# Chunk sums moved to GpSimd, and the next step's attention started inside a lone step

## What is computed

```
pooled = x.reshape(B, C, 14, 16, 14, 16).sum(axis=(3, 5))       # 16x16 patch sums
h = einsum('bcij,ce->bije', pooled, channel_weights)            # 196 tokens of 192
h = h + attention(layernorm(h))      # 12 heads; weights relu(1 + qk + qk^2 / 2), normalised
h = h + experts(layernorm(h))        # 8 experts 192 -> 768 -> 192, the best 2 of each token
```

## Time and profile before

| | |
|---|---|
| median of 3 runs | 1360.76 us (1356.45 to 1372.45) |
| span of the profiled execution | 1353.8 us |
| busy share of the span | PE 91%, PEld 81%, DVE 71%, ACT 44%, POOL 44% |
| DMA | 284.42 MB, mean 210 GB/s |
| mean granted TensorE clock | 0.937 |

### The profile page before, as it was taken

One profiled execution on the slowest core, in us unless ns is written; L12 is line 12 of the kernel. 1 busy time (PEld: TensorE's weight loads), 2 busy tenths in 40 slices (PEclk: granted clock), 3 DMA queues, 4 the chain that ended last, 5 costly groups with the idle time before them and its releaser, 6 DMA issues.

```text
span 1353.8 us, 26903 instructions
## 1 busy us (share of the span) xinstructions
PE 1228.0 (91%) x7299; PEld 1093.9 (81%) x7299; DVE 956.8 (71%) x3407; ACT 596.2 (44%) x1127; POOL 600.4 (44%) x483
## 2 busy tenths in 40 slices
PE   5867766999999999899999899999999979999997
PEld 3756655888888888788888788888888879998996
DVE  6799998787878787877787687868783523333454
ACT  1221223454545454445444354535454534544664
POOL 0104333425454454453644545464555464533433
PEclk9986556999999999898999899989999989999999
DMA  9679887767878887778786878877744655544555
GB/s 354 231 254 347 320 281 262 231 220 240 238 232 221 255 216 245 204 238 218 234 246 217 210 237 234 250 208 234 195 129 80 211 117 130 107 95 89 119 142 112
DMA packets 126551, 284.42 MB, mean 210 GB/s; under 512 B 24819, under 2 KB 70500, under 8 KB 126500
## 3 DMA queue, kind: packets, MB, share of 16 engines
q1 hardware_dynamic: 82762, 241.95, 54.5%
q0 software_dynamic: 43104, 41.25, 17.7%
q10 hardware_dynamic: 634, 0.61, 0.2%
HBM read 228.79 MB, written 54.95 MB: 210 GB/s over the span
## 4 chain that ended last, share of the span: by engine, by line
PE 33%; DMA 19%; DVE 17%; POOL 15%; issue 14%; ACT 1%; POOLq 1%; SPq 0%; ACTq 0%; DVEq 0%
PE ps L993 11%; DMA result<-ys,ridx 11%; PE ps L962 10%; POOL rows_d L608 8%; DMA rows_d<-rows,sloti 7%; POOL result L623 7%; DVE red L1069 6%; PE ps L802 3%; PE ps L933 2%; PE ps L934 2%; DMA w1r<-L_attn_w_qkv 1%; DVE stats L1197 1%; DVE topi L1206 1%; PE ps L1022 1%; DMA xr<-rows_d 1%
## 5 line engine op out<-in xcount | busy, mean ns | idle before, releaser
L623 POOL DMA_INDIRECT result<-ys,ridx x210 | 333.1, 1586 | 307.9 <-issue 120.4
L993 PE MATMUL ps<-w2a,hid 128*128 x2520 | 455.5, 327 | 0.0
L608 POOL DMA_INDIRECT rows_d<-rows,sloti x256 | 258.9, 1011 | 394.0 <-DMA rows_d<-rows,sloti 146.7
L993 PEld LDWEIGHTS ps<-w2a,hid 128*128 128x128 f32 x2520 | 415.4, 190 | 11.8 <-issue 0.2
L1069 DVE TENSOR_REDUCE red<-xbuf 128x21 f32<-128x672 f32 x448 | 359.2, 841 | 5.3 <-PE ps L866 2.4
L727 ACT ACTIVATE hid<-ps,b1s 128x512 f32<-128x512 f32 (+1 forms) x344 | 222.9, 654 | 239.2 <-PE ps L962 230.5
L962 PE MATMUL ps<-xh,w1h 128*128 128x512 f32 (+1 forms) x344 | 166.0, 482 | 7.9 <-DVE xl L1306 3.9
L1329 DVE TENSOR_TENSOR w1l<-w1r,w1h 128x768 fp32r<-128x768 f32 x116 | 110.3, 951 | 70.9 <-ACT w1h L739 70.3
L962 PE MATMUL ps<-xh,w1l 128*128 128x512 f32 (+1 forms) x344 | 131.5, 382 | 0.0
L962 PE MATMUL ps<-xb,w1h 128*128 128x512 f32 (+1 forms) x344 | 131.3, 382 | 0.0
L962 PE MATMUL ps<-xl,w1h 128*128 128x512 f32 (+1 forms) x344 | 131.2, 381 | 0.0
(11 more groups left out here) (164 smaller groups left out, 1633.8 us busy)
## 6 DMA issues: line engine op xcount, KB each, us to landing
xbuf<-x SPq DMA_DIRECT2D x224, 672.0 KB, 5.6
w1r<-L_ffn_w SPq DMA_DIRECT2D x118, 384.0 KB, 3.7
xr<-rows_d SPq DMA_DIRECT2D x48, 402.0 KB, 3.4
result<-h1s SPq DMA_DIRECT2D x32, 294.0 KB
w2a<-L_ffn_w SPq DMA_DIRECT2D x8, 576.0 KB, 7.6
rows_d<-rows,sloti POOLq DMA_INDIRECT x256
rows_d<-pad SPq DMA_DIRECT2D x9, 402.0 KB, 4.6
result<-ys,ridx POOLq DMA_INDIRECT x210, 4.9
```

The costliest lines, as they stand in the source:

```text
L608: pool.indirect_dma_start(rows_d, bass.IndirectOffsetOnAxis(ap=sloti[:, k * NT + t:k * NT + t + 1], axis=0), rows[:, t, :], None).then_inc ...
L623: pool.indirect_dma_start(out, bass.IndirectOffsetOnAxis(ap=ridx[:, b, n:n + 1], axis=0), ys[:, b, n, :], None, compute_op=ALU.add).then_i ...
L993: last = mm(yout(g, b, n), hid[:, m % 3, cols], w, start=False, stop=m == MC - 1 and n % 2 == 1)
```

## The change

Three things change, all of them ahead of the loop.

GpSimd sums some chunks: 2, 5, 8, 11 of step 0's x during the setup, the seven odd ones of step 1's x while the setup ends, then 4, 6, 9, 11 of the x of steps 2, 3 and 4 among the scatters of the lone steps 0, 1 and 2, and also 12 and 13 of step 4's x in step 3. One chunk is five additions, each of which adds the upper half of the runs to the lower half and waits for the one before. Who waits for a chunk (SP, PE) now waits for both counts.

In the lists, `T1` and `T2` now stand ahead of `S8`, the new `T3` (the next step's `S3`) behind it, and `T4` (the next step's `S4`) among the `V`s. The moments and turned features of the next step go to banks 3 to 5, its mixing to bank 7.

Four of the eight loads of `w2a` are issued in the setup ahead of the padding writes, two each in steps 0 and 1.

```diff
-STEP_ALONE = """S3 P P P P P P P P P P P P P P P P S4 S5 P P S6.0 S6.1 P S6.2 P S6.3 S7.0 P P S7.1 P P S8.0 P S8.1 P S8.2 P P S8.3
-    T1 S10 T2 R V.0 V.1 S11 V.2 V.3 S9 Q0 Q1 Q2 Q3""".split()
+STEP_ALONE = """P P P P P P P P P P P P S5 P P P P P P P P S6.0 S6.1 P S6.2 P S6.3 S7.0 P P S7.1 P P P P T1 T2 S8.0 S8.1 S8.2 S8.3
+    T3 S10 R V.0 S11 S9 V.1 T4 V.2 V.3 Q0 Q1 Q2 Q3""".split()
...
-LAST = """S3 P P P P P P P P P P S4 S5 P P P G0 G4 S6.0 S6.1 S6.2 S6.3 S7.0 P S7.1 P P G5 G1 P S8.0 S8.1 S8.2 S8.3 S10
-    R V.0 S11 V.1 V.2 S9 V.3 Q0 Q1 Q2 Q3 P P P G2 P P P P G3 P P P P""".split()
+LAST = """S5 P P P P P P G0 G4 S6.0 S6.1 S6.2 S6.3 S7.0 P P S7.1 P P G5 G1 S8.0 P P S8.1 P P S8.2 P P S8.3 S10
+    R V.0 S11 V.1 V.2 S9 V.3 Q0 Q1 Q2 Q3 P P G2 P P P P G3 P P P P P P""".split()
...
+POOL_FIRST = (2, 5, 8, 11)
+POOL_SECOND = (1, 3, 5, 7, 9, 11, 13)
+POOL_ALONE = ((4, 6), (9, 11), ())
+POOL_LONE = sum(POOL_ALONE, ())
+POOL_LAST = (12, 13)
+W2_FIRST = NE - 4
+FOLDS = EIGHTH.bit_length() - 1
...
             for k in range(CHUNKS):
-                sp.wait_ge(s_pooled, HALVES * (k + 1))
+                wait_pooled(sp, -1, k)
                 load_chunk((k + XSLOTS) // CHUNKS, (k + XSLOTS) % CHUNKS)
...
+            load_w2(0, W2_FIRST)
...
+            def P(s, k):
+
+                each, to = chunks_to(s, k)[1]
+                folds = s * (each * (FOLDS - 1)) + (to - 1) * (FOLDS - 1)
+                wait_first(pool, d_x[k % XSLOTS],
+                           (s + 1) * (16 * CHUNKS // XSLOTS) + 16 * (k // XSLOTS) + 16)
+                v = xbuf[:, k % XSLOTS].rearrange("p h n w -> p (h n) w")
+                for f in range(FOLDS):
+                    w = EIGHTH >> (f + 1)
+                    if f < FOLDS - 1:
+                        nc.gpsimd.tensor_tensor(v[:, :, 0:w], v[:, :, 0:w], v[:, :, w:2 * w], ALU.add).then_inc(s_fold, 1)
+                        wait_first(pool, s_fold, folds + f + 1)
+                    else:
+                        nc.gpsimd.tensor_tensor(red[:, k * HALVES * SUMS:(k + 1) * HALVES * SUMS].unsqueeze(2),
+                                                v[:, :, 0:w], v[:, :, w:2 * w], ALU.add).then_inc(s_pooled2, 1)
+
+            def P_group(s, group):
+
+                if group:
+                    wait_first(pool, s_mix, s + 1)
+                for k in group:
+                    P(s, k)
...
                 for t in (2 * q, 2 * q + 1):
                     if t in (3, 6):
+                        if lone[0]:
+                            P_group(s + 1, POOL_ALONE[t // 6])
                         wait_first(pool, d_scat, s * (32 * NT) + t * 32)
...
+            def G4(s):
+                P_group(s, POOL_LAST)
...
+            for k in POOL_FIRST[1:]:
+                P(-1, k)
+            P_group(0, POOL_SECOND)
             wait_first(pool, d_pad, 32)
...
             def T1(s):
-                pe.wait_ge(s_h1, s * 4 + 2)
-                S1(s + 1)
+                S1(s + 1, 7)
+
+            def T3(s):
+                S3(s + 1, 3)
+
+            def T4(s):
+                S4(s + 1)
...
                 k, h = p // HALVES, p % HALVES
+                if k in by_pool(s):
+                    return
```

More of the change, by code:

```diff
@@ L391, in factors, with by_pool, chunks_to, wait_pooled @@
             return ps[0:NF, 3 + h % FB, 0:4 * NF].rearrange("p (a b f) -> p b a f", a=2, b=2)
+        early = [True]
+        def by_pool(s):
+            if isinstance(s, int) and s < 1:
+                return POOL_SECOND if s == 0 else POOL_FIRST
+            return (POOL_LONE + POOL_LAST if isinstance(s, int) and s == PRO - 1 else POOL_LONE) if early[0] else ()
+        def chunks_to(s, k):
+            known = isinstance(s, int) and s < 1
+            each = 0 if known or not early[0] else len(POOL_LONE)
+            here = sum(q <= k for q in by_pool(s))
+            done = (0, len(POOL_FIRST))[s + 1] if known else                 len(POOL_FIRST) + len(POOL_SECOND) + (-each if each else (PRO - 1) * len(POOL_LONE) + len(POOL_LAST))
+            return (CHUNKS - each, CHUNKS + k + 1 - done - here), (each, done + here)
+        def wait_pooled(eng, s, k):
+            (a, b), (c, d) = chunks_to(s, k)
+            eng.wait_ge(s_pooled, s * (HALVES * a) + HALVES * b)
+            if c:
+                eng.wait_ge(s_pooled2, s * c + d)
+            elif d:
+                eng.wait_ge(s_pooled2, d)
         now = [0, -1]
@@ L406, in tiles_do @@
             lone[0] = not with_tiles and not last
+            early[0] = not with_tiles
             rank_bank[0] = 6 if lone[0] else 2
@@ L476, in _, with load_w2 @@
             for k in range(CHUNKS):
-                sp.wait_ge(s_pooled, HALVES * (k + 1))
+                wait_pooled(sp, -1, k)
                 load_chunk((k + XSLOTS) // CHUNKS, (k + XSLOTS) % CHUNKS)
+            def load_w2(e0, n):
+                for e in range(e0, e0 + n):
+                    sp.dma_start(w2a[:, e].rearrange("p m f -> p (m f)"), w2[e]).then_inc(d_w2, 16)
+            load_w2(0, W2_FIRST)
             set_wait(sp, "pool", "pad")
@@ L533, in S10 @@
             def S10(s):
-                if isinstance(s, int) and s < PRO - 1:
-                    for e in range(s * NE // (PRO - 1), (s + 1) * NE // (PRO - 1)):
-                        sp.dma_start(w2a[:, e].rearrange("p m f -> p (m f)"), w2[e]).then_inc(d_w2, 16)
+                if isinstance(s, int) and s < 2:
+                    load_w2(W2_FIRST + 2 * s, 2)
                 sp.wait_ge(s_h1, s * IPS + IPS)
@@ L610, in Q @@
                             rows[:, t, :], None).then_inc(d_scat, 16)
+                if q == 3 and lone[0]:
+                    P_group(s + 1, POOL_ALONE[2])
+            def G4(s):
+                P_group(s, POOL_LAST)
             def F(j, b):
@@ L865, in S1, with S3 @@
                         o = g * NTOK + hf * TOK
-                        last = mm(ps[0:TOK, 1, hf * 96:(hf + 1) * 96], red[:, o:o + TOK], mixg[:, g],
+                        last = mm(ps[0:TOK, bank, hf * 96:(hf + 1) * 96], red[:, o:o + TOK], mixg[:, g],
                                   start=g == 0, stop=g == GROUPS - 1)
                 last.then_inc(s_mix, 1)
-            def S3(s):
+            def S3(s, first=0):
                 pe.wait_ge(s_phi, s + 1)
@@ L875, in S3 @@
                         t = hf * IPS + i
-                        last = mm(ps[0:U, 0, i * NF:(i + 1) * NF], phi[:, t, 0:U], phi[:, t, :],
+                        last = mm(ps[0:U, first, i * NF:(i + 1) * NF], phi[:, t, 0:U], phi[:, t, :],
                                   start=hf == 0, stop=hf == 1)
@@ L879, in S3 @@
                 for t in range(NT):
-                    last = turn(ps[0:NF, 1 + t // IPS, (t % IPS) * TOK:(t % IPS + 1) * TOK], phi[:, t, :])
+                    last = turn(ps[0:NF, first + 1 + t // IPS, (t % IPS) * TOK:(t % IPS + 1) * TOK], phi[:, t, :])
                 last.then_inc(s_phT, 1)
@@ L1074, in _ @@
             n_early = [0]
+            ahead_of_loop = [p for p in range(PARTS) if p // HALVES not in POOL_SECOND][:7]
             def link(ins):
@@ L1080, in link @@
                 dve.wait_ge(s_dvs, n_set[0])
-            pooled = iter(range(PARTS))
+            pooled = iter([p for p in range(PARTS) if p // HALVES not in POOL_FIRST])
             def pool_first(n):
```

39 lines of the change are left out of this document (20 added, 19 removed).

## The result

The changed kernel takes 1418.77 us (median of 4 runs, 1416.93 to 1420.93) against 1362.45 us of the kernel before beside it (4 runs): 1.0418 of it, 95% interval [1.0366, 1.047]. It is 56 us slower where 27 were forecast, and lies above the range of 1350 to 1408. In a later comparison of 5 rounds (run e14) it came out at 1.0412 [1.0376, 1.0449]: 1409.27 against 1351.23 us.

A forecast was written before the change was run, and what follows sets the result against it. DVE was taken to bound the lone steps, PE the loop. Lone steps of 30.8 + 21.7 = 52.5 us and step 3's chain start the loop 27.4 us later: 1360.8 + 27.4 = 1388 us, range 1350 to 1408.

The forecast's parts named there:

- c: GpSimd's time to sum one chunk in five additions: 3.8 us; each us of it adds 14 us to the time.
- D to T: Lone step, end of `sloti` to start of next step's mixing: 30.8 us on POOL, 9 us later than DVE.
- T to D: Lone step, start of next step's mixing to end of `sloti`: 21.7 us, with `S8` at the lower clock.
- the parenthesis that gave 5.2 less: Aside on `S8` behind the next mixing: at the higher clock it would take 5.2 us less.
- Setup and step 0: Ahead of the lone steps: next mixing starts at 79 us, not 87.25; `sloti` ends at 99.5, against 100.0.
- the rival of the stops: Setup: DVE and GpSimd hold each other up, 6 us in all, giving 1394 us; inside the main case's 0.62.
- Step 3: Before the loop: scatters end at 240.3, rows load at 242.1, late chunk lands at 250.8, loop starts at 258.6.
- PE bounds behind it, so all of that stays: Loop and tail: still 1122 us, so the loop's 27.4 us later start goes fully into the time.
- DVE bounds them: Lone steps of 41.6 and 43.0 us: DVE, busy for 38.9 in each, sets their length; POOL is idle two thirds.
- a cheap sum: Rival: a chunk sum of 1.5 us gives 1356 us, or 1343 with fast `S8`; under 1347 had chance 0.12.
- The rival with c above 5.2: GpSimd's chunk sum costs more than 5.2 us; at 6.2 the time is 1422 us; chance 0.07 for above 1408.

The follow-up runs named there:

- e14: The changed kernel, unchanged, timed again beside e15 and e16 on one chip: 1409.27 us, 1.0412 of the kernel before.
- e16: The kernel before with 63 idle instructions ahead of DVE's first wait, so DVE's loop begins at 640: 1.0051 of the kernel before.
- e15: The changed kernel with 42 idle instructions ahead of DVE's first wait, so DVE's loop begins at 577 as before: 1388.44 us, 1.0277 of the kernel before.
- e8: The changed kernel without GpSimd's sums of step 1's x (DVE does them), DVE's loop at 577: 1.0277 of the kernel before.
- e11: The changed kernel with DVE, not GpSimd, summing chunks 12 and 13 of step 4's x, DVE's loop at 577: 1.019 of the kernel before.
- e13: The kernel before's order with earlier `w2a` loads; GpSimd sums only chunk 5 of each lone step's x, between scatters; DVE's loop at 577: 1.0019 of before.
- e6: The changed kernel with no GpSimd sums, only the new order and earlier `w2a` loads, DVE's loop at 577: 1.0012 of the kernel before.
- e5: The changed kernel with GpSimd summing only in setup and step 0, not in lone steps 1, 2 or step 3; DVE's loop at 577: 1.0052 of before.

## Why the prediction was wrong, point by point

Its mechanism up to the loop's start was right and its size near, partly by luck; behind the start it had nothing where there is much. On one chip (e14 to e16), 58.0 us were lost by the medians. Of them 20.8 went with the instruction packets (e14 less e15). Of the 37 left, 31 are the later start (263.6 in e15 against 232.6 in e16), and 7.5 the longer first round, both by single profiles. Without the packets the ratio of e15 on before's 1360.8 us gives 1398, inside the range of 1350 to 1408.

- **c = 3.8 us**: 4.3. My way from POOL's write rate (two reads one behind the other) gave 1.9 ns an element, the rows give 2.1; the start and wait of an addition, 0.26 in my sum, took 0.35 in the first four. The Trainium skill's GPSIMD Engine Reference, section 3.1 (about 2.6 cycles an element for want of a second read port, 2.2 ns at its 1.2 GHz), agrees with these rows; the estimate of 4.1 us made from it was the nearer one.
- **D to T 30.8 us, POOL late by 9**: 33.5 us from D to T (102.2 to 135.87, 153.1 to 186.4), PE waiting 15.0 and 14.2. Two us of the difference are c (four chunks), 0.3 the step back from a sum to a scatter (0.64 and not 0.3). DVE's last sum ahead of T ended at 125.3, 23 us behind D; 21.6 was forecast.
- **T to D 21.7 us, `S8` at the lower clock**: 17.2. `S8` was at the higher clock from its third pair, as in the parenthesis that gave 5.2 less. I had reasoned from 9 us of standing; with 15 the clock rose all the same. This error and the one before it nearly cancel, which is luck: a lone step is 50.8 us where 52.5 were forecast.
- **Setup and step 0**: T came at 84.9, not at 79, D at 102.2, not at 99.5. The difference has the size of the rival of the stops, which I had put at 6 us: DVE's scores ended 5.7 us later than before. But without the stops T still came at 83.6 (e8), and in the end they cost nothing.
- **Step 3**: the end of the scatters 243.6 (240.3 forecast), rows at 245.25 (242.1), the first chunk's sum at 252.5 (250.8), the loop at 261.2 (258.6). The chain held link by link; 30.0 us later and not 27.4. (My own sum gave 258.4: 250.8 and 7.6.)
- **"PE bounds behind it, so all of that stays", 1122 us for loop and tail**: this is the step that failed. With the packets gone it holds in sum (e15, 1122.8: first round 7.5 us longer and ten rounds 6.1 shorter than e16's), and for the kernel after it was 1144.2 (e14) and 1153.9. I took "no part of the change lies there" for "the loop runs as before". Its instructions are the same; but DVE had lost 42 ahead of them, and what that moves drew 5 packets in every round. The page of before had the row to watch, 28 packets on the instruction queue, and I had not read it as something that could change. The rest of what the loop lost, the first round, has no shown cause.
- **GpSimd's queue in step 3**: I priced chunks 12 and 13 for the mixing that waits for them, and not for the scatters of step 3 that stand behind them on POOL. e11 puts all that the two sums do at 12 us by the ratio, 4.6 of it at the loop's start.
- **"DVE bounds them"**, the premise of what could be won: DVE lost 5.7 us of work a lone step in after, and POOL's path hid it; where POOL's path did not hide it (e13), 1.3 us less brought nothing.
- **Rivals**: a cheap sum was excluded by 4.3 us a chunk. The rival with c above 5.2, 1422 us, came nearest to 1418.77 by its number, for a reason that isn't so.

Of the 58 us, then, 31 are those that the prediction was about (27.4 forecast), 21 are the packets, and the 6 or 7 left lie in the first round. What stays open: the rule of the good place; what lengthens the first round; why e6's and e5's lone steps, up to 2.7 us longer than before's, don't show in the time; and why e13's don't get shorter.

## What to carry to other kernels

Work given to an idle engine is free only in the stretch in which nobody waits for what stands behind it in its queue: list its waits first, since a wait between two groups is a hole that can be filled, and the end of the last group may be later than it looks. Two halves of a change can cost more together than apart, when one makes the late engine late and the other puts more work behind that point. And when an edit changes the number of instructions ahead of a hot loop, compare the packets on the instruction queue before reading anything else into a slower loop: a few instructions that do nothing, put where the engine stands anyway, tell whether it is that, and can give it back.
